# A gated cross-attention block: weighted row sums moved to ScalarE and Pool, attended context x W1 in place of context x W1

## What is computed

```
h   = layernorm(x)                                     # per row of 256
Sim = (h @ w1)[:, :, None] + (ctx @ w2)[:, None, :] + einsum('bid,bjd->bij', h * w3, ctx) + b_sim
A   = softmax(Sim, axis=2)
hq  = einsum('bij,bjd->bid', A, ctx)                   # attended context
Batt = softmax(max(Sim, axis=2), axis=1)               # one weight per row of h
hc  = einsum('bi,bid->bd', Batt, h)                    # weighted row sum, one vector per batch
y   = concat([h, hq, h * hq, h * hc]) @ W_qv + b_qv    # W_qv is [4 * 256, 256]: W0, W1, W2, W3
x1  = x + tanh(g_xattn) * y
out = x1 + tanh(g_ffn) * FFN(layernorm(x1))            # quantised gate and up (768), then down
```

## Time and profile before

| | us |
|---|---|
| median of the runs | 504.14 |
| the profiled execution, its own time | 504.35 |
| its span | 502.4 |
| TensorE busy, matmuls | 461.5 |
| VectorE busy | 357.1 |
| ScalarE busy | 257.0 |
| Pool busy | 42.8 |

### The profile page before, as it was taken

How to read it: one execution, slowest core, us unless ns; L and a number is a source line. 1 busy time by engine, 2 the same in 40 slices (tenths; PEclk the granted TensorE clock), 3 DMA queues, 4 the chain that set the end, 5 groups by cost and what they waited for, 6 DMA issues and landing times.

```text
span 502.4 us, 6899 instructions
## 1 busy us (share of the span) xinstructions
PE 461.5 (92%) x2506; PEld 303.5 (60%) x2506; DVE 357.1 (71%) x660; ACT 257.0 (51%) x308; POOL 42.8 (9%) x51
## 2 busy tenths in 40 slices
PE   4999999998999979989999999999859997499997
PEld 3787885987488548754444444443324443388886
DVE  6464583688257753778535469999989888899995
ACT  3795141634142200528243379999977767334430
POOL 1111111242013110300000000000100000000000
PEclk9999999998999998999999999999979999599999
DMA  8920000200020020020000000000000000233441
GB/s 249 336 73 1 0 2 12 72 1 1 0 85 0 1 83 2 0 85 0 0 0 0 0 0 0 0 1 0 1 0 0 0 0 1 84 106 129 144 146 63
DMA packets 20653, 21.09 MB, mean 42 GB/s; under 512 B 809, under 2 KB 20376, under 8 KB 20632
## 3 DMA queue, kind: packets, MB, share of 16 engines
q1 hardware_dynamic: 20612, 20.82, 13.0%
q10 hardware_dynamic: 20, 0.00, 0.0%
HBM read 12.43 MB, written 8.39 MB: 41 GB/s over the span
## 4 chain that ended last, share of the span: by engine, by line
PE 56%; issue 17%; DVE 14%; ACT 10%; POOL 1%; DMA 1%; ACTq 0%; POOLq 0%; DVEq 0%
PE ps L660 13%; PE ps L635 10%; PE ps L640 5%; PE ps L483 4%; PE ps L462 4%; PE ps L487 4%; PE ps L479 4%; ACT ag L815 3%; PE ps L525 3%; ACT hid L822 3%; PE ps L442 3%; DVE hid L1215 2%; ACT gq L810 2%; PE ps L428 1%; PE ps L451 1%
## 5 line engine op out<-in xcount | busy, mean ns | idle before, releaser
L635 PE MATMUL ps<-xh,wuh 128*128 128x512 f16 x192 | 73.5, 383 | 9.7 <-DVE gq L1240 7.8
L635 PE MATMUL ps<-xh,wul 128*128 128x512 f16 x192 | 73.3, 382 | 0.0
L640 PE MATMUL ps<-xl,wuh 128*128 128x512 f16 x192 | 57.6, 382 | 0.0
L660 PE MATMUL ps<-wdh,oh 128*128 128x256 f16 x192 | 44.9, 281 | 9.3 <-DVE oh L1277 9.3
L1187 DVE TENSOR_REDUCE cols<-hid x12 | 27.4, 2286 | 30.5 <-ACT hid L804 30.5
L660 PE MATMUL ps<-wdl,oh 128*128 128x256 f16 x192 | 44.8, 280 | 0.0
L869 ACT ACTIVATE oq<-hid,cols 128x1536 int16 (+1 forms) x16 | 25.1, 1575 | 37.3 <-DVE ol L1279 33.4
L635 PEld LDWEIGHTS ps<-xh,wuh 128*128 x192 | 18.9, 98 | 35.3 <-issue 10.9
L804 ACT ACTIVATE hid<-ps 128x2048 f32 x12 | 22.5, 1876 | 34.5 <-PE ps L640 34.5
L635 PE MATMUL ps<-xh,wgh 128*128 128x512 f16 x96 | 36.4, 379 | 0.7 <-DVE xh L1175 0.7
L635 PE MATMUL ps<-xh,wgl 128*128 128x512 f16 x96 | 36.4, 379 | 0.0
(11 more groups left out here) (179 smaller groups left out, 901.7 us busy)
## 6 DMA issues: line engine op xcount, KB each, us to landing
x_scratch<-xa SPq DMA_DIRECT2D x4, 1024.0 KB, 4.4
xo<-x_scratch SPq DMA_DIRECT2D x16, 256.0 KB, 2.8
out_dram<-xo SPq DMA_DIRECT2D x16, 256.0 KB, 2.2
xa<-in_x SPq DMA_DIRECT2D x3, 1024.0 KB, 11.8
xa<-in_x SPq DMA_DIRECT2D x4, 256.0 KB, 4.6
wv<-in_L_xattn_W_qv SPq DMA_DIRECT2D x1, 1024.0 KB, 8.2
wr<-in_L_ffn_w_gate SPq DMA_DIRECT2D x1, 768.0 KB, 10.2
wr<-in_L_ffn_w_up SPq DMA_DIRECT2D x1, 768.0 KB, 11.6
```

Of the source, the lines that this page charges most:

```text
L635: pe.matmul(ps[hf][:, q, :], w_[:, d, ds(k * P, P)], xh[:, d, n], start=d == 0 and w_ is wh, stop=False)
L640: mm = pe.matmul(ps[hf][:, q, :], wh[:, d, ds(k * P, P)], xl[:, d, n], start=False, stop=d == KD - 1)
L660: mm = pe.matmul(ps[par][:, t, 0:D], o_[:, par, k, q], w_[:, k, :], start=not low and k == 0 and w_ is wdh, stop=low and k == KF - 1)
```

## The change

- The weighted row sum leaves TensorE. ScalarE multiplies tiles 0 to 3 of a batch by their weights in place, Pool tiles 4 to 7. Pool then adds the eight tiles in four tensor_tensor instructions to one. batch_cols reads that tile (128 rows) in place of the one row, and stands behind turn_y in turns with s = 2. row_copy goes.
- project multiplies hqT with W1 (wv) in place of aT with cw. hqT is a new tile, which ScalarE copies out of PSUM (attended), and prT is made from it. context_w and context_wv go. aT shrinks to a ring of three units.
- The norm of x moves from ScalarE to VectorE, one tensor_scalar (subtract, multiply) per tile; row_shift goes.
- The bias leaves cw: VectorE makes txb = tanh(g) * b_qv once, and Pool adds it to x (bias_x(m-4), a tensor_tensor of 128 x 512 per unit), for which residual waits.
- summary moves from the end of the turns with s = 2 to the start of those with s = 3.

```diff
 # Pool
+            def row_weigh(b):
+
+                par = b % 2
+                pool.wait_ge(eb_rdy, b + 1)
+                for t in range(TB // 2, TB):
+                    i_ = pool.tensor_scalar(h[:, par, t, :], h[:, par, t, :], eb[:, t:t + 1], 1.0, ALU.mult, ALU.mult)
+                i_.then_inc(hp_rdy, 1)
+
+            def row_add(b):
+
+                par = b % 2
+                pool.wait_ge(hp_rdy, b + 1)
+                pool.tensor_tensor(h[:, par, 4:6, :], h[:, par, 4:6, :], h[:, par, 6:8, :], ALU.add).then_inc(hsum_rdy, 1)
+                pool.wait_ge(ha_rdy, b + 1)
+                pool.tensor_tensor(h[:, par, 0:2, :], h[:, par, 0:2, :], h[:, par, 2:4, :], ALU.add).then_inc(hsum_rdy, 1)
+                pool.wait_ge(hsum_rdy, 3 * b + 2)
+                pool.tensor_tensor(h[:, par, 0:2, :], h[:, par, 0:2, :], h[:, par, 4:6, :], ALU.add).then_inc(hsum_rdy, 1)
+                pool.wait_ge(hsum_rdy, 3 * b + 3)
+                pool.tensor_tensor(h[:, par, 0, :], h[:, par, 0, :], h[:, par, 1, :], ALU.add).then_inc(hs_rdy, 1)
+
+            def bias_x(n):
+
+                pool.wait_ge(h_rdy, n + 1)
+                if n == 0:
+                    pool.wait_ge(txb_rdy, 1)
+                x_ = xa[:, 2 * n:2 * n + 2, :]
+                pool.tensor_tensor(x_, x_, txb[:].unsqueeze(1).broadcast_to([P, 2, D]), ALU.add).then_inc(xb_rdy, 1)
...
                 if 1 <= m and m + 3 < N:
                     row_std(m + 3)
+                b, s = m // NP, m % NP
+                if s == 1 and 1 <= b <= B:
+                    row_weigh(b - 1)
+                    row_add(b - 1)
+                if 4 <= m < N + 4:
+                    bias_x(m - 4)
 # TensorE
-            def project(n, summed=None):
+            def project(n):
...
-                    for k in range(2):
-                        pe.matmul(o_, aT[0:JP, par, k, q], cw[0:JP, b % 3, k, :], start=k == 0, stop=False)
-                        if summed is not None:
-                            row_sum(summed, 4 * t + k)
+                    for d in range(KD):
+                        pe.matmul(o_, hqT[:, par, d, q], wv[:, KD + d, :], start=d == 0, stop=False)
                     for d in range(KD):
                         pe.matmul(o_, prT[:, par, d, q], wv[:, 2 * KD + d, :], start=False, stop=False)
-                        if summed is not None:
-                            row_sum(summed, 4 * t + 2 + d)
...
             def batch_cols(b):
 
-                pe.wait_ge(hrow_rdy, b + 1)
+                pe.wait_ge(hs_rdy, b + 1)
                 for d in range(KD):
-                    pe.matmul(m_bank[:, HC + d:HC + d + 1], hrow[0:1, d * P:(d + 1) * P], ones[0:1, 0:1], start=True, stop=True)
+                    pe.matmul(m_bank[:, HC + d:HC + d + 1], h[:, b % 2, 0, d * P:(d + 1) * P], ones[:, 0:1], start=True, stop=True)
...
-                pe.wait_ge(cw_rdy, min(b + 2, B))
+                pe.wait_ge(cbi_rdy, min(b + 2, B))
 # ScalarE
+            def attended(n):
+                b, s, par = place_of(n)
+                act.wait_ge(hq_ps, n + 1)
                 ge(act, f_ps, n - 2 * NP + 1)
+                act.activation(hqT[:, par, :, s * PT:(s + 1) * PT], hq_bank.rearrange("p (d n) -> p d n", d=KD),
+                               ACT.Copy).then_inc(hqT_rdy, 1)
...
+            def row_weigh(b):
+
+                act.wait_ge(eb_rdy, b + 1)
+                for t in range(TB // 2):
+                    a_ = act.activation(h[:, b % 2, t, :], h[:, b % 2, t, :], ACT.Copy, scale=eb[:, t:t + 1])
+                a_.then_inc(ha_rdy, 1)
...
-                if m + 1 < N:
-                    norm_x(m + 1)
...
+                if 3 <= m <= N + 2:
+                    attended(m - 3)
+                if s == 1 and 1 <= b <= B:
+                    row_weigh(b - 1)
 # VectorE
+            def norm_x(n):
...
                 dve.wait_ge(rstd_rdy, n + 1)
+                ge(dve, hc_ps, b - 1)
+                for t in range(2 * s, 2 * s + 2):
+                    c = par * TB + t
+                    i_ = dve.tensor_scalar(h[:, par, t, :], xa[:, b * TB + t, :], mv[:, par, t, 0:1], rstd[:, c:c + 1],
+                                           ALU.subtract, ALU.mult)
+                i_.then_inc(h_rdy, 1)
...
-                dve.wait_ge(hq_ps, n + 1)
+                dve.wait_ge(hqT_rdy, n + 1)
...
-                dve.tensor_tensor(prT[:, par, :, q], hq_bank.rearrange("p (d n) -> p d n", d=KD), hT[:, par, :, q],
-                                  ALU.mult).then_inc(pr_rdy, 1)
+                dve.tensor_tensor(prT[:, par, :, q], hqT[:, par, :, q], hT[:, par, :, q], ALU.mult).then_inc(pr_rdy, 1)
...
                 dve.wait_ge(f_ps, n + 1)
+                dve.wait_ge(xb_rdy, n + 1)
...
+                if s == 3 and 1 <= b <= B:
+                    summary(b - 1)
                 if m == 0:
-                    row_shift(3)
...
+                    norm_x(3)
+                if 3 <= m and m + 1 < N:
+                    norm_x(m + 1)
```

More of the change, by code:

```diff
@@ L146, in build @@
     hT = place(a, "hT", [P, 2, KD, S], F32)
-    aT = place(a, "aT", [JP, 2, 2, S], F32)
+    hqT = place(a, "hqT", [P, 2, KD, S], F32)
     prT = place(a, "prT", [P, 2, KD, S], F32)
@@ L158, in build @@
     cx = [cx01[:, 0], cx01[:, 1], cx23[:, 0], cx23[:, 1]]
-    cw = place(a, "cw", [JP, 3, 2, D], F32)
+    aT = place(a, "aT", [JP, 3, 2, PT], F32)
     a = copy_of(r_wd)
@@ L167, in build @@
     wrow = place(a, "wrow", [3 * KD, P], F32)
-    bqb = place(a, "bqb", [P, D], F32)
-    hrow = place(copy_of(r_wu), "hrow", [1, D], F32)
+    txb = place(a, "txb", [P, D], F32)
     a = copy_of(r_tmp)
@@ L411, in context_bias @@
                 mm.then_inc(cbi_ps, 1)
-            def context_w(b):
-                pe.wait_ge(cbi_rdy, b + 1)
-                pe.wait_ge(wqv_in, 16)
-                for k in range(2):
[L417 to L420, removed]
             def turn_h(n):
@@ L574, in _ @@
                 if LAG <= m and not late:
-                    project(m - LAG, b - 1 if s == 2 and 1 <= b <= B else None)
+                    project(m - LAG)
                 if s == 1 and 1 <= b <= B and LAG <= m:
@@ L585, in _ @@
                     score(m - 1)
[L586 to L589, removed]
                 if 2 <= m <= N + 1:
@@ L593, in _ @@
                     batch_max(b - 1)
-                if s == 2 and 1 < b <= B:
-                    batch_cols(b - 1)
                 if 3 <= m <= N + 2:
                     attend(m - 3)
-                if s == 2 and b == 1:
-                    batch_cols(b - 1)
                 if LAG < m:
                     turn_y(m - LAG - 1)
+                if s == 2 and 1 <= b <= B:
+                    batch_cols(b - 1)
                 if s == 3 and b + 1 < B:
                     context_bias(b + 1)
[L604 to L607, removed]
                 if LAG <= m and late:
@@ L680, in _ @@
             act.activation(c_t2, c_g3[:, 0:2], ACT.Tanh).then_inc(tanh_rdy, 1)
[L682 to L686, removed]
-                    c = par * TB + t
-                    a_ = act.activation(h[:, par, t, :], xa[:, b * TB + t, :], ACT.Identity,
-                                        bias=nmr[:, c:c + 1], scale=rstd[:, c:c + 1])
-                a_.then_inc(h_rdy, 1)
             def turned_h(n):
@@ L970, in last_y @@
             def last_y():
+                dve.wait_ge(xb_rdy, N)
                 for t in range(2):
@@ L1017, in summary @@
                 ge(dve, f_ps, NP * (b - 1))
+                if b == 0:
+                    dve.wait_ge(wqv_in, 16)
                 for d in range(KD):
@@ L1114, in _ @@
                     batch_shift(b - 1)
-                if s == 2 and b == 1:
-                    row_copy(b - 1)
-                if 2 <= m and m + 2 < N:
-                    row_shift(m + 2)
-                if s == 2 and 1 < b <= B:
-                    summary(b - 1)
                 if m in W_AT:
```

70 lines of the change are left out of this document (23 added, 47 removed).

## The result

The changed kernel takes 517.09 us (median of 4 runs, 515.90 to 518.16), the kernel before 504.08 in the same job. The ratio is 1.0256, its 95% interval 1.0230 to 1.0282: slower by 13 us, where 492.0 was forecast and 500 was the end of the range. The profiled execution took 518.16 us, its span 516.4.

A forecast was written before the change was run, and what follows sets the result against it. TensorE was taken to bound the kernel up to 217 us. Gains of 3.0 to step 7, 6.6 to projection 9 and 5.5 to projection 12 made 15.1, less 3 for clock: 12.1 us, so 492.0 us, range 479 to 500.

The forecast's parts named there:

- the waits of the new path: TensorE's new waits at batches 0 to 3 and behind them, before the FFN: 12.9 + 4.2 + 4.4 us.
- What goes: TensorE's removed work: laced row sums 17.3, batch 0's row sums 3.5, context x W1 6.9, in all 27.7 us.
- ScalarE and VectorE: ScalarE's load about even; VectorE about +4 us, 1.5 us idle per step for hqT, 0.5 us per step contention with Pool.
- Pool: Weighing 0.6 us each, adds and bias 1.05 at 512 elements; 6.5 us per batch and 16.8 us of bias.
- Batch 0: No projection covers it: eb 3.3 us sooner than 37.4, sum 6.5 later at 40.6, small matmuls end at 41.4.
- Batch 1, the chain: From batch_max's start T: row_std released at T + 12.1, sum at T + 19.3, wanted at T + 13.8: wait 5.5 us.
- Batch 1, what follows: Behind Pool's late bias and y_std: turn_a 1.2 us more, we 1.3 us.
- Batch 2: From batch_max's start T: eb at T + 6.9, sum at T + 15.5; wait 1.9 us, then turn_a waits 3.0.
- Batch 3, eb at T + 2.9 and no wait: T is batch_max's start; sum 6.2 us after eb, wanted at T + 10.4; behind it y_std 2.0, we 2.2 late.
- Clock: "-3": New waits over 2 us at batches 0, 1 and 2 each bring a slow clock stretch of 1.7 us: -3 us.
- VectorE becomes the bound throughout: Rival, chance 0.08: contention 1 us a step more than assumed over steps 8 to 15, 4 us gain left, 500 us.
- The rival on the slower side: Chance 0.05: Pool's 16 weighings slow batch_cols; slower from 1.6 us each, 509 us at 2.0 each.

The follow-up runs named there:

- experiment 9: The kernel before with the eight row sums of batches 1 to 3 in one run instead of laced into the projection: 493.49 us, ratio 0.9804.
- experiment 5: The changed kernel with the 16 bias instructions on Pool left out, so the output lacks the bias: 508.24 us, 1.0087 of the kernel before.
- experiment 8: The changed kernel with 33 filler matmuls, results unread, where TensorE stood idle in front of its waits: 509.13 us, 1.0104 of the kernel before.
- experiments 7: The changed kernel with prT made by VectorE from PSUM, ahead of ScalarE's copy hqT: 507.23 us, 1.0052 of the kernel before.

## Why the prediction was wrong

Its sum was 12.1 us of gain, the profile shows 14.0 of loss: 26.1 us off. Two steps failed, with about the same weight: the waits of the new path, 21.5 us forecast and 33.2 measured, where it left out what stands behind Pool's chain (the summary and turn_context, batch 1) and that VectorE is late in batch 3 too, and the clock behind these waits (3 us forecast for the new stretches, 1.3 net of what goes; 13.0 measured). The steps, in the order of the prediction:

- *What goes* (27.7 us) was right. The projections of the changed kernel take 5.2 us in every step at full clock (170.62 to 175.8). The laced sums, put at 17.3 us, are 3 x 5.76 by experiment 9.
- *ScalarE and VectorE.* Right in kind: the wait for hqT was put at 1.5 us a step and is 1.28 in most steps (14 waits, 18.3 us in all); contention with Pool was foreseen and is there. Its price, 0.5 us in each of 16 steps, is about what experiment 5 shows: 6.7 us of VectorE's busy time (4.9 in norm_x1, 1.1 in the norm of x, 14.6 to 13.5, and 0.7 in the summary, 5.5 to 4.8). With the +4 of moved work the forecast had some 12 us more for VectorE; it is 14.8. What was missed is that the lateness stays: it was counted for batches 1 and 2 and left out for batch 3.
- *Pool.* The weighing at 0.6 was 0.515 (16 of them, 8.0 us). The adds and the bias, set at 1.05, are 1.26 to 1.38: the line through two larger shapes was too low at 512 elements. The adds (0.726 us at 256, 1.268 at 512) lie on a steeper line than weight_q and weight_n, 2.1 ns per element; why is open.
- *Batch 0*: failed in part. The chain from eb was put at 6.5 us and took 10.3 (35.7 to 46.05): a row_std stood in front on Pool, which VectorE released only at 38.26 and which ended at 39.05, and one add took 1.71 beside VectorE. eb itself was put at 34.1, counted from 37.4, where the trace of before has the end of L753 at 36.5. The wait was 7.70 us, forecast 4.4.
- *Batch 1, the chain*: right. T + 10.9 and T + 18.2 against T + 12.1 and 19.3; 4.28 us against 5.5.
- *Batch 1, what follows*: failed. Turn_a and we were given 1.2 and 1.3 us. That the summary now stands behind norm_x1, and turn_context behind the summary, was not seen: 5.91 us.
- *Batch 2*: right in size, 1.99 and 2.94 against 1.9 and 3.0, with 0.76 that wasn't listed; here VectorE's lateness was counted (eb at T + 8.0, put at T + 6.9).
- *Batch 3, eb at T + 2.9 and no wait*: the clearest miss. eb came at T + 7.2, since VectorE was behind by then too (its prT of that step starts 0.8 us after T); the sum was late by 3.52 us, and turn_y and the projection waited 4.74 and 1.37 behind it, forecast 2.0 and 2.2. The prediction let VectorE start batch 3 on time, though it had it 4 us late one batch earlier. T + 2.9 was too early even for the kernel before, which has eb at T + 3.8 (T 166.08):

```profile
169.55 0.30 ACT L753 ACTIVATE cols<-cols 128x8 f32<-128x8 f32 x1 [4.80 <-DVE cols L1005]
```

- *Clock: "-3"*: the largest miss by size. It counted 1.7 us per wait from the earlier trace rows, less 1.7 for what goes. The low stretches here last 10 to 13.7 us, not 3.4, and cost 13.0 more than before.

In a sum: new waits 33.2 us in place of 21.5 (11.7), smaller waits up by 2.8, the clock 13.0 in place of 1.3 (11.7). That is 26.2 of the 26.1.

TensorE: Matmul & The Clock Gate (the Trainium skill, "HAM oscillation — how this bites in real kernels") works out the penalty as half of all the throttled time. By it the added 47.9 us would cost 24. This trace says 13, since TensorE stood idle in 21 of the 53.6 us, which are counted as waits; experiment 8 gave back 8.0.

The rival "VectorE becomes the bound throughout" (500 us) came nearest, since VectorE's lateness is the cause: experiments 7 and 5 give back 9.9 and 8.9 us by the wait for hqT and by the bias on Pool. But its own term, contention of 1 us a step more than assumed, didn't come (6.7 us in all, where the sum already held some 8), and VectorE is no bound throughout: it is busy 151 of the 239 us, and what is late is its place in the chain. No rival had what TensorE's waits do to its clock. The rival on the slower side (Pool's weighing) was wrong outright. How the 11.7 us of the table divide over W1 on hqT, the bias and the norm was not run with laced sums and stays open. Nor was Pool's queue reordered, with y_std ahead of the weighings or the bias and weight_q behind it, which would say what the queue alone costs.

## What to carry to other kernels

Work taken off the bounding engine is worth what it removes only while its new path ends before the engine asks: list for each new wait what the in-order queue in front and behind holds, and carry lateness on from batch to batch. Before moving work to another engine, try its place on its own: the same row sums in one run, one stage later and no longer laced, brought 10.6 us with no other part changed, 6.7 of it from not lacing. Where a change gives TensorE new waits close to one another, bound the low clock behind them by the whole stretch up to the last of them, not by the shortest stretch that a busier trace shows.

## What the hardware showed

- *The clock.* Three of the four long stretches begin inside a wait (of 7.70, 4.28 and 3.52 us), one behind waits of 1.99 and 0.76; further waits of 5.91, 2.94 and 4.74 us fall into three of them. The granted clock then stayed at 1.2 GHz for 10.2 to 13.7 us; before the change it had been 3.4 us each time. With fillers in the waits it stayed at 2.4 GHz from 20 us to the FFN but for one stretch of 3.4 us.
- *Lacing.* Row sums between the projection's matmuls, with their weights of one column, cost 5.76 us for eight; in one run 3.54 (experiment 9, batch 1).
- *VectorE beside Pool.* In the changed kernel two pieces of VectorE's work beside Pool's (an addition of 128 x 2 elements, 0.17 us where Pool is idle, and norm_x1, 0.73 us for the pair there), VectorE first, then Pool:

```profile
169.84 2.63 DVE L966 TENSOR_SCALAR cols<-cols 128x2 f32<-128x2 f32 x1
...
193.81 2.77 DVE L972 TENSOR_SCALAR yb<-xa,cols 128x256 f32<-128x256 f32 x2 [4.17 <-issue]
```

```profile
169.68 2.78 POOL L374 TENSOR_TENSOR wr<-wr,wsc 128x1536 f32<-128x1536 f32 x1 [3.65 <-ACT wr L764]
...
193.69 1.26 POOL L402 TENSOR_TENSOR xa<-xa,txb 128x512 f32<-128x512 f32 x1
194.91 1.53 POOL L368 TENSOR_TENSOR wr<-wr,wri 128x768 f32<-128x768 f32 x1
```

VectorE's instruction on two elements per partition ends with Pool's on 1536 beside it (172.47 and 172.46). SBUF — State Buffer (the Trainium skill, "Who interferes with whom") says that tensor_scalar can run in a mode that takes the ports which VectorE shares with Pool, that the engine which issues first keeps them for its whole instruction, and that the other is blocked, not slowed; these rows agree.
